# Output of ten second-layer head groups sent by transfers instead of being turned on TensorE, in a two-layer attention kernel

## The reference

```python
# layer 0 (no mask)
xm = rms(x) * (1 + scale) + shift            # scale, shift from cond @ w_cond
q, k, v = split(xm @ w_qkv);  q, k = rope(q), rope(k)
o = softmax(q @ k.T * 16 ** -0.5) @ v        # per head
x = o @ w_out + x
# layer 1 (mask over keys)
xn = layer_norm(x)
q, k, v = xn @ q_w + q_b, xn @ k_w + k_b, (xn @ v_w + v_b) * mask
y = softmax(q @ k.T + (1 - mask) * -1e6) @ v # per head
h = layer_norm(y) * (1 + scale) + shift      # scale, shift from silu(cond) @ emb_w
x = x + silu(h) @ out_w + out_b
```

## Time and profile before

| | |
|---|---|
| median of 3 runs | 490.78 us (490.25 to 492.41) |
| profiled execution | 490.88 us |
| its span | 488.7 us |
| granted TensorE clock | 1.000 of full over the span |
| PE busy | 477.4 us, 98% |
| DVE busy | 385.4 us, 79% |
| ACT busy | 342.1 us, 70% |
| POOL busy | 313.7 us, 64% |

### The profile page before, as it was taken

How to read it: one execution, slowest core, us unless ns; L and a number is a source line. 1 busy time by engine, 2 the same in 40 slices (tenths; PEclk the granted TensorE clock), 3 DMA queues, 4 the chain that set the end, 5 groups by cost and what they waited for, 6 DMA issues and landing times.

```text
span 488.7 us, 9702 instructions
## 1 busy us (share of the span) xinstructions
PE 477.4 (98%) x3197; PEld 179.5 (37%) x3197; DVE 385.4 (79%) x989; ACT 342.1 (70%) x677; POOL 313.7 (64%) x445
## 2 busy tenths in 40 slices
PE   7999899999999999999999999999999999999996
PEld 3553322322443325332443335334333323333234
DVE  3767896999886796958886698866899999999124
ACT  2662467898667785968667785876787788777853
POOL 5569976899885996789755791859990055005501
PEclk9999999999999999999999999999999999999999
DMA  7775157454522465216502361113311121111011
GB/s 251 201 202 192 45 152 250 112 150 128 150 61 65 129 178 151 62 33 181 154 19 69 113 179 45 46 45 113 106 46 44 45 89 45 44 46 45 1 44 44
DMA packets 41577, 49.79 MB, mean 102 GB/s; under 512 B 12388, under 2 KB 34036, under 8 KB 41272
## 3 DMA queue, kind: packets, MB, share of 16 engines
q1 hardware_dynamic: 33336, 31.84, 21.8%
q0 software_dynamic: 7904, 16.03, 11.3%
q10 hardware_dynamic: 288, 1.31, 0.8%
HBM read 27.62 MB, written 19.01 MB: 95 GB/s over the span
## 4 chain that ended last, share of the span: by engine, by line
PE 79%; DVE 12%; POOL 3%; issue 2%; ACT 1%; DVEq 0%; POOLq 0%; ACTq 0%
PE bank L596 20%; PE bank L642 12%; PE bank L570 12%; PE bank L579 11%; PE bank L558 9%; DVE masked L955 7%; PE bank L653 6%; PE bank L670 5%; DVE row_max L958 2%; PE bank L627 2%; POOL XN L930 1%; PE bank L611 1%; PE bank L604 1%; ACT probs L780 1%; PE bank L727 1%
## 5 line engine op out<-in xcount | busy, mean ns | idle before, releaser
L780 ACT ACTIVATE probs<-bank 128x512 f32<-128x512 f32 x512 | 269.2, 601 | 71.1 <-PE bank L570 70.3
L958 DVE TENSOR_REDUCE row_max<-bank 128x1 f32<-128x512 f32 x256 | 159.4, 681 | 34.0 <-PE bank L579 33.7
L579 PE MATMUL bank<-k_s,q_s 64*128 64x512 f16 x512 | 178.3, 382 | 2.0 <-DVE row_max L958 1.2
L955 DVE CUSTOM_DVE_ANT_0 masked<-bank,mask_bias 128x512 bf16<-128x512 f32 x256 | 161.8, 687 | 19.3 <-PE bank L579 18.7
L558 PE MATMUL bank<-q_s,k_s 64*128 64x512 f16 x512 | 151.5, 380 | 0.3
L570 PE MATMUL bank<-shift,kx 64*128 64x512 f16 x512 | 148.8, 376 | 0.0
L596 PE MATMUL bank<-probs,v_aug 128*17 128x512 f32 x1024 | 135.4, 598 | 0.7 <-ACT probs L780 0.7
L579 PEld LDWEIGHTS bank<-k_s,q_s 64*128 64x128 f16 x512 | 46.2, 93 | 156.1 <-DVE row_max L958 70.2
L642 PE MATMUL bank<-xT,wqkv 128*128 128x512 f32 x128 | 59.6, 605 | 1.1 <-DVE xT L1096 0.6
L1236 POOL TENSOR_SCALAR scaled<-row_max 128x16 f32<-128x16 f32 x30 | 7.7, 256 | 81.4 <-DVE row_max L955 45.1
L570 PEld LDWEIGHTS bank<-shift,kx 64*128 64x128 f16 x512 | 46.8, 95 | 33.6 <-DMA shift<-shift_rows 0.4
(11 more groups left out here) (123 smaller groups left out, 478.7 us busy)
## 6 DMA issues: line engine op xcount, KB each, us to landing
q_s<-q_parts SPq DMA_DIRECT2D x32, 256.0 KB, 3.0
k_s<-k_parts SPq DMA_DIRECT2D x32, 256.0 KB, 3.7
k_parts<-parts POOLq DMA_DIRECT2D x62, 128.0 KB, 3.0
...
O<-oT SPq DMA_DIRECT2D x64, 32.0 KB, 2.2
...
```

The source lines that it names most:

```text
L579: nc.tensor.matmul(bank, m.q_s[slot][rows, i, queries], m.k_s[slot][rows, i, :], start=True, stop=True).then_inc(q.d_made, 1)
L780: act.activation(m.probs[k][:, h, :], bank, ACT.Exp, scale=1.0 if s >= B * NG else float(DH) ** -0.5)\
L955: dve.tensor_tensor_reduce(m.masked[D["max", n, k, h] % ND][:, :], bank, m.mask_bias[:, b, :], 1.0, LOWEST, ALU.add, ALU.max, to)\
L958: dve.tensor_reduce(to, bank, AX.X, ALU.max).then_inc(q.d_done, 1)
```

## The change

The outputs of groups 16 to 25 no longer are turned on PE. They go by transfers as in layer 0: `SENT` is 26, and `sums`, `raw_output`, `invert`, `inverses_out`, `inverses_in` run up to it. POOL divides the five pairs in place (`divide(4, 0)` to `divide(6, 0)`; the argument counts batches over both layers). Since the statistics want tokens by rows, each pair is then turned back by a new piece `back` (four transposes, A ring) and copied by ACT into `tokens` (the memory of `wc`, free by then). Groups 26 to 30 still are turned on PE.

ACT's copy of ACC for groups 17 to 26 now waits until the transfers of the group before have landed (`output_out`, `sums_in`), where it waited for PE's turn.

The pieces move: `qk` chunks 2 and 3 of batch 3 (layer 0) go together into (1, 2); `back` stands in (20, 1), (21, 3), (23, 3), (25, 2) and (28, 2); the value piece of the last batch goes from (20, 3) to (21, 3); the turns of batch 0 from group 22 to 23, of batch 1 from 26 to 27; the two halves of `y(1, 0)`, in (23, 2) and (24, 3), go together into (25, 3), those of `y(1, 1)`, in (27, 2) and (28, 3), into (28, 3). The statistics of batches 0, 1 and 2 go from (20, 3), (24, 3), (28, 3) to (21, 3), (25, 3), (28, 3). POOL's list is rewritten.

PE, groups 23 to 24 of before: the second half of `y(1, 0)` (L670), with plain steps around it (L596 is `values`, L579 `max`, L558 `score`, L570 `shift`).

The diff, cut where only names, waits of the same kind or declarations change:

```diff
--- before.py
+++ after.py
...
@@ -92,7 +95,7 @@
 
 PIECES = {
     0: ((), qk(0, 3, 1), (), ()),
-    1: (qk(0, 3, 2), (), qk(0, 3, 3), ()),
+    1: ((), (), qk(0, 3, 2, 3), ()),
     2: ((), (), (), (("embed", 1),)),
 }
 
@@ -103,13 +106,13 @@
     PIECES[_s] = ((), y(0, _b), v(1, _b - 1) if _b else v(0, 3), ())
     PIECES[_s + 1] = ((), (), turn("p1", _b), qk(1, _b, 0, 1))
     PIECES[_s + 2] = ((), qk(1, _b, 2, 3), (), ())
-PIECES[20] = ((), qk(1, LAST, 2, 3), (), v(1, LAST))
-PIECES[22] = (*one(turn("f1", 0)), (), ())
-PIECES[23] = ((), (), y(1, 0)[:1], ())
-PIECES[24] = ((), (), (), y(1, 0)[1:])
-PIECES[26] = (*one(turn("f1", 1)), (), ())
-PIECES[27] = ((), (), y(1, 1)[:1], ())
-PIECES[28] = ((), (), (), y(1, 1)[1:])
+
+PIECES[20] = ((), qk(1, LAST, 2, 3) + (("back", 0, 0),), (), ())
+PIECES[21] = ((), (), (), (("back", 0, 1),) + v(1, LAST))
+PIECES[23] = (*one(turn("f1", 0)), (), (("back", 1, 0),))
+PIECES[25] = ((), (), (("back", 1, 1),), y(1, 0))
+PIECES[27] = (*one(turn("f1", 1)), (), ())
+PIECES[28] = ((), (), (("back", 2, 0),), y(1, 1))
 PIECES[30] = (*one(turn("f1", 2)), (), ())
 PIECES[31] = ((), *one(y(1, 2)), ())
 
@@ -117,8 +120,8 @@
 STATISTICS = {}
 for _b in range(B):
     STATISTICS[6 + NG * _b, 2] = ("p1", _b)
-for _b in range(B - 1):
-    STATISTICS[20 + NG * _b, 3] = ("f1", _b)
+for _b, _s in enumerate((21, 25, 28)):
+    STATISTICS[_s, 3] = ("f1", _b)
 
 
 PAIRS = TPB // 2
@@ -159,7 +162,7 @@
 
 
 HIGH_BEHIND = [("qk", 0, 0, 2), ("qk", 0, 0, 3), ("turn", "p0", 1, 1), ("v", 0, 0, 1)]
-OUT_AT = {25: 0, 29: 1, 32: 2}
+OUT_AT = {26: 0, 29: 1, 32: 2}
 
 
 USES = [("p0", 0), ("p0", 1), ("p0", 2), ("p0", 3), ("f0", 0), ("p1", 0), ("f0", 1), ("p1", 1), ("f0", 2), ("p1", 2),
@@ -189,9 +192,9 @@
                 yield ("statistics",) + STATISTICS[s, k]
             for piece in PIECES.get((s, k), ()):
                 yield "piece", piece
-        if op == "output" and k == 2 and s > LAYER:
+        if op == "output" and k == 2 and s > SENT:
             yield op, s - 1
-        if op == "output" and k == 3 and 0 < s <= LAYER:
+        if op == "output" and k == 3 and 0 < s <= SENT:
             yield "sums", s - 1
         if op == "maxima" and k == TURNED and exists(s + 1):
             yield op, s + 1
...
@@ -367,6 +370,9 @@
         m.wqkv = [sb(f"wqkv{i}", [P, CT, 3 * C]) for i in range(2)]
         m.wo = [sb(f"wo{i}", [P, CT, C]) for i in range(2)]
         m.wc = sb("wc", [P, KC, COND])
+
+        m.tokens = [m.wc[:, 2 * i:2 * i + 2, :].rearrange("p k n -> p (k n)").rearrange("p (t c) -> p t c", c=C)
+                    for i in range(2)]
         m.vb_row = sb("vb_row", [P, C])
         m.ob_row = sb("ob_row", [P, C])
         m.vecs = sb("vecs", [P, VECS])
...
@@ -627,6 +633,14 @@
             last = nc.tensor.transpose(bank[:, t * P:(t + 1) * P], src[:, t, h * P:(h + 1) * P], m.ident[:, :])
         last.then_inc(q.d_made if for_dve(piece) else q.a_made, 1)
 
+    def turn_back(piece):
+        _, b, c = piece
+        bank = a_free(A[piece])
+        pe.wait_ge(q.divided, normalised(B + b, c))
+        for t in range(TPB):
+            last = nc.tensor.transpose(bank[:, t * P:(t + 1) * P], m.raw[b % 2][:, c, t * P:(t + 1) * P], m.ident[:, :])
+        last.then_inc(q.a_made, 1)
+
     def queries_keys(piece):
         _, layer, b, i = piece
         use = USES.index((("p0", "p1")[layer], b))
...
@@ -782,7 +798,7 @@
 
     def copy_output(s):
         act.wait_ge(q.values_done, KT * (s + 1))
-        if s > LAYER:
+        if s > SENT:
             act.wait_ge(q.d_made, D["output", s - 1] + 1)
         elif s:
             act.wait_ge(q.output_out, group_out(s - 1))
@@ -820,6 +836,14 @@
             act.activation(to, bank, ACT.Identity, bias=m.vecs[:, NORM_B + h:NORM_B + h + 1],
                            scale=m.vecs[:, NORM_W + h:NORM_W + h + 1]).then_inc(q.a_done, 1)
 
+    def back(piece):
+        _, b, c = piece
+        bank = made(A[piece])
+        if b >= 2:
+            act.wait_ge(q.xn_made, TPB * NORMAL.index(("f1", b - 2)))
+        act.activation(m.tokens[b % 2][:, :, c * P:(c + 1) * P], bank.rearrange("p (t n) -> p t n", n=P), ACT.Copy)\
+            .then_inc(q.a_done, 1)
+
     def conditions(piece):
         bank = made(A[piece])
         if piece[0] == "embed":
...
@@ -977,17 +1003,15 @@
     def write_output(s):
         pu, g = divmod(s, NG)
         bank = made(D["output", s]).rearrange("p (t h w) -> p t h w", t=KT, h=G)
-        if s == LAYER:
-            dve.wait_ge(q.inv_out, 16 * LAYER)
-        if g == 0 and pu < B + 2:
-            dve.wait_ge(q.divided, normalised(pu - 2, CT - 1))
-        if g == 0 and pu >= B + 2:
+        if s == SENT:
+            dve.wait_ge(q.inv_out, 16 * SENT)
+        if s == SENT or g == 0:
             dve.wait_ge(q.xn_made, TPB * NORMAL.index(("f1", pu - 2 - B)))
-        if s > LAYER:
+        if s > SENT:
             dve.wait_ge(q.d_done, D["output", s - 1] + 1)
         dve.reciprocal(m.inv_sum[:, :, :, :], bank[:, :, :, DH:DH + 1]).then_inc(q.inv_made, 1)
         dve.wait_ge(q.inv_made, s + 1)
-        dve.tensor_tensor(m.O[pu % 2][:, :, g * G * DH:(g + 1) * G * DH].rearrange("p t (h d) -> p t h d", d=DH),
+        dve.tensor_tensor(m.tokens[pu % 2][:, :, g * G * DH:(g + 1) * G * DH].rearrange("p t (h d) -> p t h d", d=DH),
                           bank[:, :, :, 0:DH], m.inv_sum[:, :, :, :].broadcast_to([P, KT, G, DH]), ALU.mult)\
            .then_inc(q.d_done, 1)
 
@@ -1016,8 +1040,10 @@
             dve.wait_ge(q.d_done, D["y", 0, b, 1] + 1)
             statistics(kind, b, lambda t: m.X[:, TPB * b + t, :])
         else:
-            dve.wait_ge(q.d_done, D["output", NG * (B + b) + NG - 1] + 1)
-            statistics(kind, b, lambda t: m.O[b % 2][:, t, :])
+            dve.wait_ge(q.a_done, max(A[piece] for piece in A if piece[:2] == ("back", b)) + 1)
+            if NG * (B + b) + NG > SENT:
+                dve.wait_ge(q.d_done, D["output", NG * (B + b) + NG - 1] + 1)
+            statistics(kind, b, lambda t: m.tokens[b % 2][:, t, :])
         aggregate(kind, b)
 
     def opening():
...
@@ -1309,14 +1335,17 @@
                                m.v_bias[:, :].rearrange("p (h d) -> p h d", d=DH),
                                m.v_tmp[:, t, :].rearrange("p (h d) -> p h d", d=DH), ALU.add).then_inc(q.v_made, 1)
 
-    def divide(b, c):
-
-        use = USES.index(("f0", b))
-        pool.wait_ge(q.output_out, group_out(NG * b + 2 * c + 1))
-        pool.wait_ge(q.inv_in[c], 32 * (b + 1))
-        await_read(pool, q, use - 2)
-        pool.tensor_tensor(m.xT[use % 2][:, c, :], m.raw[b % 2][:, c, :], m.inverse[c][:, :], ALU.mult)\
-            .then_inc(q.divided, 1)
+    def divide(pu, c):
+
+        layer, b = divmod(pu, B)
+        pool.wait_ge(q.output_out, group_out(NG * pu + 2 * c + 1))
+        pool.wait_ge(q.inv_in[c], 32 * (pu + 1))
+        to = raw = m.raw[b % 2][:, c, :]
+        if layer == 0:
+            use = USES.index(("f0", b))
+            await_read(pool, q, use - 2)
+            to = m.xT[use % 2][:, c, :]
+        pool.tensor_tensor(to, raw, m.inverse[c][:, :], ALU.mult).then_inc(q.divided, 1)
 
     moments_order = []
     for op, *at in order():
@@ -1455,31 +1484,48 @@
         negate(NG * b + 11)
         if b == 1:
             modulation()
-    normalise(LAST)
-    add_output_bias(LAST)
-    add_bias(LAST - 1, 0)
-    add_bias(LAST - 1, 1)
-    negate(NG * LAST + 9)
-    for i in range(4):
-        split(B + LAST, i)
-
-    for b in range(LAST):
-        negate(NG * (B + b) + 6)
-        rstd("f1", b)
-        normal("f1", b)
-        if b == 0:
-            add_bias(LAST, 0)
-        negate(NG * (B + b) + 7)
-        if b == 0:
-            add_bias(LAST, 1)
+    def silu(b):
         for h in range(CT):
             i, h = silu_ready(pool, q, ("turn", "f1", b, h))
             pool.tensor_scalar(m.tanh[h], m.tanh[h], 1.0, None, ALU.add).then_inc(q.tanh_step, 1)
             pool.wait_ge(q.tanh_step, CT * b + h + 1)
             pool.tensor_tensor(m.xT[i][:, h, :], m.tanh[h], m.halved[h], ALU.mult).then_inc(q.silu_made, 1)
-        for n in (NG * (B + b) + 8, NG * (B + b) + 9):
-            if n in POOL_SHIFTS:
-                negate(n)
+
+    normalise(LAST)
+    divide(B, 0)
+    add_output_bias(LAST)
+    add_bias(LAST - 1, 0)
+    add_bias(LAST - 1, 1)
+    negate(21)
+    split(B + LAST, 0)
+    split(B + LAST, 1)
+    negate(22)
+    divide(B, 1)
+    split(B + LAST, 2)
+    split(B + LAST, 3)
+    negate(23)
+    rstd("f1", 0)
+    normal("f1", 0)
+    negate(24)
+    divide(B + 1, 0)
+    silu(0)
+    negate(25)
+    add_bias(LAST, 0)
+    negate(26)
+    divide(B + 1, 1)
+    add_bias(LAST, 1)
+    negate(27)
+    rstd("f1", 1)
+    normal("f1", 1)
+    negate(28)
+    divide(B + 2, 0)
+    silu(1)
+    negate(29)
+    negate(GROUPS - 2)
+    rstd("f1", 2)
+    normal("f1", 2)
+    negate(GROUPS - 1)
+    silu(2)
     for p in range(PAIRS):
         at = slice(2 * p, 2 * p + 2)
```

(19 more changed lines are left out.)

10 lines of the change are left out of this document (5 added, 5 removed).

## The result

| | before | after |
|---|---|---|
| median | 490.82 us (8 runs, 490.25 to 494.49) | 487.94 us (8 runs, 487.21 to 488.91) |
| ratio to before | | 0.9931, 95% interval 0.9906 to 0.9956 |
| profiled execution's span | 488.7 us | 486.4 us |
| granted TensorE clock over the span | 1.000 | 1.000 |
| PE / DVE / POOL busy | 477.4 / 385.4 / 313.7 us | 474.5 / 380.9 / 320.0 us |

What follows compares the result with a forecast made beforehand. PE was taken to bound the kernel, 98% busy, with DVE having next to no slack in a 2.48 us plain step. Terms summed to -1.99 us from 490.88, forecast median 488.8; own range 488.0 to 489.6, 8 in 10 487.0 to 491.9.

Steps and rivals of the forecast that it cites:

- the lone turn back: Turn back standing alone in (23, 3), A ring: priced like two token turns, +1.06 us; other bound 0.62.
- the wait in (25, 2): PE's turn back waits 1.5 us (0.3 to 1.9) for group 23's inverses and POOL's division; step +2.12 us.
- Ten output turns, -5.69: Steps (17, 2) to (26, 2) lose their turns: seven lone at 0.62, three beside other pieces at 0.45 us.
- What would show it: Signs listed beforehand; right: plain 2.5 us steps in 17, 20, 21, 24, 25, 26 and about 4.6 in (25, 2).
- Pairing w_out, -0.42: Four w_out halves at 1.94 us, 7.76, become two wholes at 3.67, 7.34: -0.42 us.
- the stall behind the statistics, -0.66: The 0.33 us PE stall after a w_out half with statistics goes twice, for batches 1 and 2: -0.66 us.
- rival A: No wait in (25, 2): chain 5.2 us or less, step costs 1.06, sum -3.05, 487.7 us; chance 0.25.
- Three turns back beside other work, +1.35: Turns back in (20, 1), (21, 3), (28, 2), beside qk chunks, value piece, output turn: 0.45 us each.
- Inversions, +0.35: Ten inversions of sums on DVE in the second layer; five in plain steps cost 0.07 us each.
- qk pair, -0.10: Two qk chunks paired in (1, 2) save one entry into a piece: -0.1 us, half of 0.21.
- Cost 0 for POOL, the statistics' wait, ACT's copy: Five POOL divisions, statistics waiting in (21, 3) under the value piece, ACT's ACC copy waiting for transfers: no added time.
- Rivals B and C: B: longer chain, 8.5 us, to (25, 2), 490.5 us, chance 0.21. C: ACT's copy waits for transfers, 493.8 us, 0.11.

Runs made afterwards that it cites:

- experiment 1: The changed kernel with the turn back of groups 22 and 23 moved from (25, 2) to beside the w_out piece in (25, 3): 486.54 us, ratio to before 0.9921.
- Experiment 3: The kernel before with the new table of pieces, statistics and POOL list, but nothing sent, all second-layer outputs turned on PE: 489.60 us, ratio 0.9971.
- experiment 2: The kernel before with only the w_out halves of y(1, 0) and y(1, 1) paired, in (24, 3) and (28, 3): 490.15 us, ratio 0.9983.
- experiment 7: Experiment 1's kernel with POOL's last operand split for batches 1 and 2 put behind the division: 486.58 us, ratio to before 0.9913.
- Experiment 5: The changed kernel with SP first writing group 23's inverses to a second place in DRAM and waiting until that landed: 488.17 us, one run.
- experiments 3 and 6: 6: the changed kernel with an extra one-input DVE statistics instruction in each of steps (17, 2) to (26, 2): 488.23 us, one run. 3 has its own line.

## Why the prediction was right, and where not

The mechanism was the forecast one, and most terms held in the steps to a tenth or better. The two largest errors were both on the cautious side: the lone turn back (0.46 too dear) and the wait in (25, 2) (0.86 too dear). Mainly through them the sum was -1.99, where the steps outside (14, 0) show -3.27. That is why the time came out below the forecast's own range and below the 488.3 that I had called faster, with a chance of 0.37.

- *Ten output turns, -5.69.* Right: six of the seven lone steps fell from 3.12 (3.42 in groups 22 and 26, where the delay of the token turns' DVE work moved with the turns) to 2.5. The seventh, (25, 2), holds a turn back now, and is 2.51 in experiment 1, where that is gone. Two of the three beside other pieces fell by 0.43 and 0.44. Experiment 3 against the changed kernel shows the sending apart from the moves. (The list under "What would show it" names 25 among the plain steps and leaves out 22; it should be the other way round.)
- *Pairing w_out, -0.42, and the stall behind the statistics, -0.66.* Right for batch 1, 0.18 too much for batch 2. A half beside an output turn costs 1.76, not 1.94, and with the stall the pairing gives 0.37 per batch by itself (experiment 2). In batch 1 the turn beside the half goes as well, and I had given the discount to the turn (0.45 instead of 0.62), so the two terms together are right. In batch 2 the turn in (27, 2) stays: the steps there gave 0.36, where the sum had 0.54.
- *Lone turn back in the A ring, +1.06.* Wrong by 0.46: it cost 0.60 in (23, 3). I had taken the release of the second exponential as its bound, from two turns that ended with it by chance. Counting banks: with one turn between, the second of the next two scores takes the bank four places back, which is the *first* exponential's, and that is free by then. The rows above bear it out: the score starts 0.16 us before the second exponential ends. The 1.06 of two turns is PE's own time, as (28, 2) shows: turn back in the A ring and output turn in the D ring take 3.54 together.
- *The wait in (25, 2), 1.5 us.* It was there and it was the critical place, but 0.6 us: the chain took 5.90 us, not 6.8. In the changed kernel all five divisions of the second layer follow their inversion after 5.74 to 6.19 us. The other bound of the trace, 5.49, was the nearer one. Most of the difference to the neighbour that I chose (7.08) lies in the write of the inverses: the read back was issued 2.83 us after the inversion there, and 387.10 - 385.27 = 1.83 us here. In group 11 POOL issued four operand transfers of 128 KB beside that write; that they delayed it is likely and not tested. POOL's own work also ended only 0.02 us before that division (at 233.68), so 7.08 need not be the transfers' time alone: in experiment 7, where POOL stood idle for 3.58 us ahead of it, group 11's chain was 232.70 - 226.22 = 6.48, with the read back still issued 2.80 us after the inversion. The step cost 3.74 - 2.48 = +1.26, not 2.12; the forecast had named 4.6 us as the sign of being right and 3.5 as that of rival A. Experiment 5 shows that the wait is paid one for one, experiment 1 what is left on the table by its place.
- *Three turns back beside other work, +1.35.* 0.44, 0.39 and 0.42 in (20, 1), (21, 3) and (28, 2), together 1.25.
- *Inversions, +0.35; qk pair, -0.10.* 2.55 us in the steps as forecast; the pair gives 0.2.
- *Cost 0 for POOL, the statistics' wait, ACT's copy.* Held. In (21, 3) the statistics waited for the copy under the value piece, and the step was 6.53, less than the 6.60 of a value piece with an output turn.

With the measured sizes the sum is -1.99 - 0.46 - 0.86 - 0.10 (turns back) - 0.10 (qk pair) + 0.18 (batch 2's pair) = -3.33, against -3.27 in the steps outside (14, 0) and -2.9 in the median. Rival A was nearer in size (-3.05) but had not the mechanism: there was a wait of 0.6 us, and the lone turn in (23, 3) did not cost 1.06. Rivals B and C did not happen; the raw outputs landed early enough everywhere. The page "DMA: Bandwidth & Descriptors" of the Trainium skill (section "Anatomy of one DMA") gave 4.3 us for the two transfers. The page fits it to transfers that GpSimd issues, and these are issued by SP. The chain of 5.90 us less the inversion (0.25) is 5.65, so its fixed cost plus bytes is short here by 1.35 us, while my 6.8 for the whole chain was 0.90 too long.

What stays open: what delays the shift rows of group 14. The step was 0.2 to 1.0 us longer in five profiles, of the kernel before as well, and not in the other five; two of those (experiments 3 and 6) have such a wait in (10, 0) instead, of 0.56 and 0.04 us. Competing transfers are the likely cause, but experiment 7 does not show it.
